# Zero-padding two 48-row operands of the third expert layer to 128 rows

## What is computed

```
# x: [512 tokens of a group, 128]; h = layernorm(x)
scores = sigmoid(normalised(h) @ normalised(gate_w).T)        # 16 per token
w      = scores where in the top 8, else 0;  w /= sum(top 8)  # routing weights
for e in 16 experts:
    y += w[:, e] * ((silu(h @ w_gate[e]) * (h @ w_up[e])) @ w_down[e])
y += (silu(h @ sw_gate) * (h @ sw_up)) @ sw_down              # shared expert
x = x + y
```

## Time and profile before

| | |
|---|---|
| three executions | 670.77, 673.10, 673.24 us; median 673.1 us |
| profiled execution | 671.91 us, with a span of 670.1 us from the first to the last instruction |
| busy: PE / PEld | 561.8 us (84%) / 370.8 us (55%) |
| busy: DVE / ACT / POOL | 467.6 us (70%) / 260.0 us (39%) / 98.5 us (15%) |
| mean granted TensorE clock | 0.971 |

### The profile page before, as it was taken

The page is one execution under the profiler, slowest core; times in us unless marked ns, Lnnn a source line. Parts: engine busy times, 40 slices in busy tenths (PEclk is TensorE's granted clock), DMA queues, the critical chain, the costliest instruction groups (busy, mean ns, idle before and its releaser), DMA issues.

```text
span 670.1 us, 11020 instructions
## 1 busy us (share of the span) xinstructions
PE 561.8 (84%) x4434; PEld 370.8 (55%) x4441; DVE 467.6 (70%) x1200; ACT 260.0 (39%) x422; POOL 98.5 (15%) x101
## 2 busy tenths in 40 slices
PE   1426689878999999988998889998799978998787
PEld 0425255668455755665776755556345654566435
DVE  7688888775588677765247646886653487876785
ACT  1365544324345334435332542543321024452270
POOL 5021210004410141000002015100100012002120
PEclk9967999998999999999999999999999999999989
DMA  8900000000000000000000000000000000000001
GB/s 279 391 0 2 0 2 1 1 1 1 1 1 1 2 1 1 2 1 0 1 2 0 1 1 1 1 2 1 0 1 0 1 1 0 2 2 0 1 0 32
DMA packets 6722, 12.43 MB, mean 19 GB/s; under 512 B 528, under 2 KB 4880, under 8 KB 6288
## 3 DMA queue, kind: packets, MB, share of 16 engines
q1 hardware_dynamic: 6672, 11.73, 4.9%
HBM read 11.21 MB, written 0.52 MB: 18 GB/s over the span
## 4 chain that ended last, share of the span: by engine, by line
PE 59%; DVE 23%; ACT 11%; POOL 2%; issue 2%; DMA 1%; SPq 1%; DVEq 0%; ACTq 0%
PE ps L399 43%; PE ps L461 11%; ACT big L938 5%; DVE st L1206 3%; PE ps L415 3%; PE ps L477 2%; DVE xn L1403 2%; POOL rs L332 2%; DVE big L1317 1%; DVE mx L1313 1%; DVE x L1330 1%; DMA co<-in_ctx 1%; DVE mv L1209 1%; PE ps L604 1%; DVE ve L1211 1%
## 5 line engine op out<-in xcount | busy, mean ns | idle before, releaser
L938 ACT ACTIVATE big<-ps 128x1024 f32<-128x1024 f32 x80 | 81.8, 1024 | 108.7 <-PE ps L461 108.7
L1313 DVE TENSOR_REDUCE mx<-ps 128x8 f32<-128x1024 f32 x80 | 97.5, 1219 | 27.8 <-PE ps L399 27.8
L1317 DVE TENSOR_TENSOR big<-ps,mx 128x1024 f32<-128x1024 f32 x80 | 98.0, 1225 | 6.9
L399 PE MATMUL ps<-bt 128*128 128x512 bf16 (+1 forms) x361 | 94.0, 369 | 9.1 <-DVE ve L1211 3.1
L461 PEld LDWEIGHTS ps<-kt,big 128*128 128x128 f32 x640 | 71.0, 141 | 39.3 <-DVE big L1317 28.6
L461 PE MATMUL ps<-kt,big 128*128 128x128 f32 x640 | 85.2, 276 | 5.9 <-DVE big L1317 5.9
L332 POOL TENSOR_TENSOR rs<-ve,negh 128x4 f32<-128x4 f32 x26 | 26.4, 1016 | 381.1 <-DVE ve L1211 381.1
L399 PE MATMUL ps<-xnT,wt 128*128 128x512 f32 (+1 forms) x140 | 66.5, 602 | 4.8 <-DVE big L1595 2.6
L399 PEld LDWEIGHTS ps<-wt,big 128*128 128x128 f32 (+1 forms) x480 | 56.0, 191 | 8.5 <-issue 7.9
L399 PE MATMUL ps<-big,vaug 128*32 128x128 f32 x1280 | 51.5, 279 | 10.8 <-ACT big L938 10.8
L399 PE MATMUL ps<-wt,big 128*128 128x128 f32 (+1 forms) x480 | 60.3, 279 | 0.0
(11 more groups left out here) (275 smaller groups left out, 741.4 us busy)
## 6 DMA issues: line engine op xcount, KB each, us to landing
wt<-in_weights SPq DMA_DIRECT2D x1, 1664.0 KB, 16.2
wt<-in_weights SPq DMA_DIRECT2D x1, 1603.0 KB, 11.1
wt<-in_weights SPq DMA_DIRECT2D x6, 256.0 KB, 10.2
bt<-in_bconsts SPq DMA_DIRECT2D x1, 1024.0 KB, 7.6
rowt<-in_rows SPq DMA_DIRECT2D x1, 975.0 KB, 5.9
wt<-in_weights SPq DMA_DIRECT2D x1, 832.0 KB, 12.7
wt<-in_weights SPq DMA_DIRECT2D x1, 608.0 KB, 17.3
wt<-in_weights SPq DMA_DIRECT2D x1, 580.0 KB, 5.4
```

What stands on the lines that cost most here:

```text
L399: return pe.matmul(out, lhsT, rhs, start=start, stop=stop, **k)
L938: act.activation(PT[:, half * HH:(half + 1) * HH, :].rearrange("p (i j) k -> p i j k", i=2), heads_of(pair(g, half)), ACT.Exp, scale=SCALE ...
L1313: dve.tensor_reduce(top, S, AX.X, ALU.max).then_inc(*s.step())
L1317: dve.tensor_tensor(pr[:, half * HH:(half + 1) * HH, :].rearrange("p (i j) k -> p i j k", i=2), S, top.unsqueeze(3).to_broadcast([P, 2, HG ...
```

## The change

Both tables get 128 partitions instead of 48. GpSimd fills them with zeros once in the preamble, ahead of `vaug` and `vv`: `pairs` (128 x 1024 bfloat16) once, and `gwsT` (128 x 512 bfloat16) for each of the two groups. The writes that fill rows 0 to 47 stay as they are but name those rows, and VectorE waits for the zeros of `pairs` before it writes. The 16 spreading products take all 128 rows of both operands, 80 of which are zero.

```diff
-    pairs = sb("pairs", [3 * E2, E2 * HE2], BF16)
+    pairs = sb("pairs", [P, E2 * HE2], BF16)
...
-            self.gwsT = own("gwsT", [3 * E2, W4], BF16)
+            self.gwsT = own("gwsT", [P, W4], BF16)
...
         pool.memset(tiny[:, :], 1e-10).then_inc(*p.step())
+        pool.memset(pairs[:, :], 0.0).then_inc(*p.step("no_pairs"))
         for t in tiles:
+            pool.memset(t.gwsT[:, :], 0.0).then_inc(*p.step())
             pool.memset(t.vaug[:, :, :, :], 1.0).then_inc(*p.step("vaug"))
             pool.memset(t.vv[:, :, :, :], 1.0).then_inc(*p.step("vv"))
...
-                            read(t.gwsT[:, :], bank(2).bitcast(BF16)[0:3 * E2, 0:W4], "gwsTp", "gwsT")
+                            read(t.gwsT[0:3 * E2, :], bank(2).bitcast(BF16)[0:3 * E2, 0:W4], "gwsTp", "gwsT")
...
-            dve.tensor_copy(pairs[:, :].rearrange("p (e k) -> p e k", e=E2),
+            dve.wait_ge(*p.at("pre.no_pairs"))
+            dve.tensor_copy(pairs[0:3 * E2, :].rearrange("p (e k) -> p e k", e=E2),
                             const("ident3")[0:3 * E2, :].unsqueeze(2).to_broadcast([3 * E2, E2, HE2])).then_inc(*p.step("pairs"))
```

## The result

| | before | after |
|---|---|---|
| five executions, side by side | 670.17 to 673.24 us, median 670.77 | 665.74 to 668.88 us, median 666.26 |
| profiled execution (its span) | 671.91 us (670.1) | 668.88 us (667.1) |
| mean granted TensorE clock in it | 0.971 | 0.968 |

The ratio is 0.9937 with a 95% interval of 0.9913 to 0.9961: the change makes the kernel 4.2 us faster, between 2.6 and 5.8. The forecast was 3.1 us less and 669.4 us. The gain forecast lies in that interval; the time doesn't fit: 666.26 lies 3.1 us under it and 0.7 under the lower end of the range. The profiled execution of after is the slowest of its five, so its stages are read for where time goes, not its total for how much.

A forecast was written before the change was run, and what follows sets the result against it. TensorE's time in the layer `L2f` was taken to bound the kernel. Spreads at -4.5 us and fills at +1.4 us gave -3.1 us, from 672.5 to 669.4 us, range 667.0 to 672.6 us.

The forecast's parts named there:

- The layer bounds itself on TensorE: In L2f the chain stays on TensorE for 45.48 us, so time taken from TensorE there comes off the end.
- 0.30 us per spread, 4.5 us in all: In L2f, 128 rows cut the period from 3.13 to 2.83 us for 13 spreads; the other three gain less.
- The two spreads behind the 64-column weights: Two spreads after chunk 8 still change shape on entry, so they gain 0.20 us each instead of 0.30.
- A change of shape stops the load, a change of type doesn't: TensorE's weight loads start ahead across a type change but not a shape change, so 128 rows remove the loss.
- Row counts don't matter to a load: Skill rule cited as counter-evidence: a load's time follows columns, not rows; by that alone padding gains nothing.
- The rival of no gain: Late loads in L2f have another cause, 128 rows don't mend them, only the fills count: 673.9 us, chance 0.10.
- 1.8 us of fills, 0.3 hidden, 1.4 in the chain: At the start, GpSimd's three fills take 1.8 us and delay its first root; slack hides 0.3, 1.4 lengthens the chain.
- The rival of the nearly free start: Fills go by bytes or unseen slack hides them, costing only 0.5 us at the start: 668.5 us, chance 0.20.
- 669.4 us and the range: Whole kernel: 3.1 us less than 672.5, the middle of four executions; range 667.0 to 672.6 us, forecast's chance 0.60.
- the clock rival: Low-clock stretches come or go as stages move, 1.7 us either way; no chance given, others widened by about 1.2 us.

The follow-up runs named there:

- the run with 48 rows and a short layer: Kernel with only the fills (48-row spreads), one of four down products left out in chunks 0 to 7, spreads cut to 368 columns: 666.21 us, ratio 0.9925.
- The refilled layer: The change with each of 16 spreading products preceded by two extra ones, of 200 and 512 columns, writing the same values: 669.92 us, ratio 1.0015.

## Why the prediction was right and wrong

- **The layer bounds itself on TensorE**: right. The chain stays on TensorE for the whole piece, before and after.
- **0.30 us per spread, 4.5 us in all**: right to the second digit, 4.50 us. The parts hold too: period 2.83 us, load 0.43 us ahead. The two spreads behind the 64-column weights kept their late entry (0.81 us idle) until the run that padded those weights took it away.
- **A change of shape stops the load, a change of type doesn't**: right for what the kernel does, too narrow in words. 96 rows against 128 is a change of shape and costs next to nothing; 64 rows do cost.
- **Row counts don't matter to a load**: the rule quoted against the change holds for the duration of a load (0.09 to 0.10 us at 48, 64, 96 and 128 rows) and says nothing of when it may start. The rival of no gain (673.9 us) is out: the run with the fills alone reads 48 rows of the same wide tables, with the same waits, and stays at 45.48 us.
- **1.8 us of fills, 0.3 hidden, 1.4 in the chain**: right. 1.82 us, 1.50 in the chain, 1.6 in the total of the run with the fills alone. One detail was off: VectorE's rounding ends last, at 19.05, and not ScalarE's, which I had at 18.9. The rival of the nearly free start, which came nearest to the measured time, fell in that run: it was near for a wrong reason.
- **669.4 us and the range**: wrong, and this has two parts. First, the sum was set off from 672.5, the middle of four executions of which three lay high; the median of before is 670.6 to 671.1 in the runs that followed. That is 1.7 us of the miss of 3.1, and it was bad luck in a small sample that the prediction took at face value. Second, the clock rival: I gave it "no case of its own, as it acts both ways" and 1.2 us. That step failed. The low clock cost 2.75 us in one stage and 1.64 in another, and 3.3 us went there between two profiled executions. Executions of one kernel spread over 5 us (665.43 to 670.56), and kernels fall into groups some 3 to 5 us apart, in shares that change from kernel to kernel: 14 of all 17 executions of the change are in the lower one (665.4 to 666.4), 6 of all 60 of before (667.4 to 668.7, none of them in the first comparison or on the third chip). An edit that moves the stages can therefore change the median by the shift and by a change of shares, here about 1 to 2 us in favour. On the chip where the change ran again the lower groups alone differ by 2.6 us (medians 665.8 and 668.4, the second of only four executions), which is near the sum of 3.0. The remaining 1.4 us of the miss is, by this account, of that kind; for single executions without a profile it is argued from their times, not read from stages.

That it comes from the place of the stages is shown as far as the run with 48 rows and a short layer goes. It isn't settled what decides an execution's group. The refilled layer had its stages nearly where the run with only the fills had them, and still had seven of twelve executions at 669.2 to 670.0 where the other, on another chip, had one of twelve at 670.3 and the rest from 671.9 up. Their profiles show where most of it went, first for the fills alone (672.77 us), then for the refilled layer (669.23 us):

```profile
640.52 12.36 PE ps L401 x20
```

```profile
640.02 9.31 PE ps L401 x20
```

The same 20 records take 3.05 us more in the first, with a granted clock of 0.56 between 639.0 and 646.4 us, against 1.00 between 635 and 648 in the second. Why the clock was low in one and not in the other no run has tested. The mean granted clock of a whole execution doesn't tell the groups apart either: before has executions of 670 us at 0.991, the change has its quick ones at 0.976. That fits a low clock costing time only where the chain is on TensorE, but no run has tested it.

## What to carry to other kernels

Read the weight loads of TensorE beside the products: a load that starts with its own product, after idle time that waits for nothing, is one that wasn't taken ahead, and here it cost its own length (0.10 us) once on entry and twice on the way back. Where one operand of 64 rows or fewer stands alone among products of 128, zero rows cost no time on TensorE and win it back (96 rows did nearly as well as 128 here); fill them where the filling engine is idle, not ahead of the first step that others wait for. And read an edit of a few microseconds from its stages: two profiled executions of the same kernel differed here by 3.3 us, in stages where their clocks differ.

## What the runs showed of the hardware

- The loss depends on a class of row counts: 48 and 64 rows among 128-row products cost 0.30 us each time (layer 45.48 us), 96 rows next to nothing (41.05 against 40.98). A 64-column stationary operand among 128-column ones costs too: the load behind it had 0.81 us of idle time before it, and 0.24 once the operand was padded. Padding the two of them and the operands of 64 rows together gained 0.68 us in this loop (40.98 to 40.30); no run parts the columns from the rows.
- On when a load may run ahead, one sentence of the Trainium skill, "TensorE: Matmul & The Clock Gate", section "The mechanism", has loads overlap running products only when their row groups differ. Here loads of 128 rows run during products of 128 rows and start 0.43 us ahead of their own; the loads that don't are those whose rows or columns differ in class. The measurement decides.
- GpSimd fills bfloat16 at the rate per element of float32: 1024 elements in 0.88 us from start to start, 2048 float32 in 1.75.
